# Turned maxima share a ring buffer with the row sums, the FFN runs as one burst, the absolute maximum is taken by halves

## What is computed

```
def proj(W):
    y = jnp.einsum('oc,bct->bto', W, x)
    return y.reshape(B, T, H, Dh).transpose(0, 2, 1, 3)
Q, K, V = (proj(Wq), proj(Wk), proj(Wv))
att = jnp.einsum('bhqd,bhkd->bhqk', Q, K) * (1.0 / math.sqrt(Dh))
att = att + b[0]
m = mask[:, None, None, :]
att = att * m + (1.0 - m) * NEG_INF
att = jax.nn.softmax(att, axis=-1)
y = jnp.einsum('bhqk,bhkd->bhqd', att, V)
...
absmax = jnp.max(jnp.abs(x), axis=-1, keepdims=True)
scale = jnp.maximum(absmax, eps) / 127.0
q = jnp.clip(jnp.round(x / scale), -128, 127).astype(jnp.int8)
...
acc = jnp.einsum('bsk,nk->bsn', q, weight, preferred_element_type=jnp.int32)
out = acc.astype(jnp.float32) * in_scale * w_scale[:, 0] + bias
return out.astype(jnp.float16)
```

## Time and profile before

| | |
|---|---|
| median of 3 runs | 2563.82 us |
| profiled execution, its own time | 2565.66 us |
| its span | 2563.9 us |
| mean granted TensorE clock | 0.991 |
| TensorE, VectorE, ScalarE, GpSimd busy | 96%, 56%, 56%, 72% |
| L131, row maximum 128x1024, x1024 | 1220 ns |
| L911, absolute maximum 128x1024, x32 | 1212 ns |
| L914, L916 (128x1), x32 each | 154, 164 ns |
| L921, product 128x512, x64 | 751 ns |
| L807, exp 128x512, x2048 | 603 ns |
| L974, y 128x512, x64 | 1281 ns |
| L967, addition 128x2048, x254 | 4582 ns |

### The profile page before, as it was taken

The page is one execution under the profiler, slowest core; times in us unless marked ns, Lnnn a source line. Parts: engine busy times, 40 slices in busy tenths (PEclk is TensorE's granted clock), DMA queues, the critical chain, the costliest instruction groups (busy, mean ns, idle before and its releaser), DMA issues.

```text
span 2563.9 us, 40963 instructions
## 1 busy us (share of the span) xinstructions
PE 2455.4 (96%) x12880; PEld 1354.0 (53%) x12880; DVE 1448.3 (56%) x1459; ACT 1435.3 (56%) x2664; POOL 1853.0 (72%) x614
## 2 busy tenths in 40 slices
PE   8999999979999999999999999999999999999996
PEld 7888888864444444444444444444444444444442
DVE  3211111156666666667666666666666666666660
ACT  3222222216656666666666666666666666666664
POOL 3332222227878888888888888888888888888885
PEclk9999999989999999999999999999999999999998
DMA  6655545633333333433333333333333343433311
GB/s 246 255 194 196 196 188 188 207 133 84 89 81 92 89 85 88 95 84 84 84 95 85 84 84 84 84 84 84 84 84 93 92 95 92 90 93 85 86 41 34
DMA packets 151511, 282.62 MB, mean 110 GB/s; under 512 B 30489, under 2 KB 66329, under 8 KB 151393
## 3 DMA queue, kind: packets, MB, share of 16 engines
q10 hardware_dynamic: 49312, 130.80, 22.8%
q1 hardware_dynamic: 102080, 150.57, 16.8%
HBM read 178.29 MB, written 101.45 MB: 109 GB/s over the span
## 4 chain that ended last, share of the span: by engine, by line
PE 58%; DVE 8%; issue 7%; POOL 2%; ACT 2%; DMA 1%; DVEq 0%; ACTq 0%; POOLq 0%; SPq 0%
PE score L703 17%; PE ring L122 16%; PE pv L730 15%; DVE neg_max L131 7%; PE ring L762 4%; PE ring L740 4%; PE ring L743 2%; DVE absmax L911 1%; POOL acc L967 1%; ACT probs L807 1%; POOL y L974 0%; DMA sums<-recips_by_head 0%; DMA recips<-sums 0%; DVE scale L914 0%; POOL k_stack L116 0%
## 5 line engine op out<-in xcount | busy, mean ns | idle before, releaser
L131 DVE TENSOR_REDUCE neg_max<-ring 128x1 f32<-128x1024 f32 x1024 | 1219.0, 1220 | 572.6 <-PE ring L122 570.0
L807 ACT ACTIVATE probs<-score 128x512 f32<-128x512 f32 x2048 | 1104.0, 603 | 378.3 <-PE score L703 357.9
L967 POOL TENSOR_TENSOR acc<-acc,probs 128x2048 f32<-128x2048 f32 x254 | 1163.7, 4582 | 17.4 <-ACT probs L807 0.2
L703 PE MATMUL score<-q_stack,k_stack 100*128 100x512 f32 x2048 | 882.5, 433 | 27.9 <-ACT probs L807 15.2
L122 PE MATMUL ring<-k_stack,q_stack 98*128 98x512 f32 x2048 | 825.1, 403 | 46.3 <-DVE neg_max L131 41.9
L703 PEld LDWEIGHTS score<-q_stack,k_stack 100*128 100x128 f32 x2048 | 387.7, 190 | 489.8 <-ACT probs L807 349.1
L730 PE MATMUL pv<-probs,v_in 128*32 128x512 f32 x4096 | 546.3, 605 | 0.0
L122 PEld LDWEIGHTS ring<-k_stack,q_stack 98*128 98x128 f32 x2048 | 390.6, 191 | 150.3 <-DVE neg_max L131 90.7
L967 POOL TENSOR_TENSOR acc<-probs 128x2048 f32<-128x2048 f32 x64 | 292.6, 4572 | 150.1 <-ACT probs L807 150.1
L474 POOL TENSOR_TENSOR q_stack<-x_raw,k_stack 128x1024 fp32r<-128x1024 f32 x28 | 67.7, 2450 | 293.5 <-ACT k_stack L359 293.5
L730 PEld LDWEIGHTS pv<-probs,v_in 128*32 128x32 f32 x4096 | 80.6, 108 | 185.9 <-issue 106.3
(11 more groups left out here) (90 smaller groups left out, 1888.7 us busy)
## 6 DMA issues: line engine op xcount, KB each, us to landing
k_stack<-qk_part ACTq DMA_DIRECT2D x93, 512.0 KB
q_stack<-qk_part ACTq DMA_DIRECT2D x183, 256.0 KB, 3.9
qk_part<-part_hi SPq DMA_DIRECT2D x64, 512.0 KB, 2.6
qk_part<-part_lo SPq DMA_DIRECT2D x64, 512.0 KB, 3.5
v_steps<-v_out SPq DMA_DIRECT2D x64, 256.0 KB, 2.2
sums<-recips_by_head SPq DMA_DIRECT2D x64, 256.0 KB
res<-x ACTq DMA_DIRECT2D x32, 512.0 KB, 4.5
out<-res SPq DMA_DIRECT2D x64, 256.0 KB, 4.7
```

Source lines behind the costliest of these rows:

```text
L131: nc.vector.tensor_reduce(neg_max[:, pair // CHUNK, pair % CHUNK:pair % CHUNK + 1], ring[:, :], AX_X, ALU.max, negate=True).then_inc(neg_m ...
L703: pe.matmul(score[score_bank(t)][:, :], k_stack[par][0:ROWS, h, kt * P:(kt + 1) * P], q_stack[par][0:ROWS, half, h, :], start=True, stop=T ...
L807: nc.scalar.activation(probs[:, kt, h, :], score[score_bank(t)][:, :], ACT.Exp).then_inc(exp_done, 1)
L967: nc.gpsimd.tensor_tensor(acc[:, half, :, :], first, probs[:, k, :, :], ALU.add).then_inc(acc_done, 1)
```

## The change

- Turned maxima are written to columns 512 to 639 of the ring buffer that takes the sums; sums and turn are one extra: chunk 1 with the sums of (s-1, half 1) at unit 23, chunk 0 of s+1 with the sums of (s, half 0) at unit 55. The turn comes first.
- The turning of q goes from unit 41 to 51. The FFN's 16 matmuls are one extra at unit 59 on both banks of one buffer, with the two products behind them. Extras per step are 4 instead of 7.
- The absolute maximum is taken by halves, at units 27 (with a maximum against EPS, `take_floor`) and 39, and the scale follows there; recip of (s-1, half 1) goes from 17 to 31. round_rows goes from 31, 32 to 41, 42; make_ints from 36, 37 to 43, 44; take_qT from 42, 43 to 52, 53; load_res from 14 to 30.
- SP stores chunk 1 of the maxima ahead of the sums' gather, and gathers (s, half 0) after the store of chunk 0.
- GpSimd: normalise half 0 after the first addition, half 1 after the fourth, finish after the eighth, then two more. The last step adds in half 1 as before.

```diff
-SUMS_1, TURN_1, TURN_Q, FFN_0, FFN_1, SUMS_0, TURN_0 = 11, 23, 41, 45, 49, 51, 55
-EXTRAS = (SUMS_1, TURN_1, TURN_Q, FFN_0, FFN_1, SUMS_0, TURN_0)
+SUMS_1, TURN_Q, SUMS_0, FFN = 23, 51, 55, 59
+EXTRAS = (SUMS_1, TURN_Q, SUMS_0, FFN)
...
             def step(s, par, prev=True, main=True, ahead=True):
-                if prev:
-                    gather_sums(s - 1, 1)
-                    spread_recips(s - 1, 1)
                 if main:
                     sp.wait_ge(max_hi_done, 2 * s + 2)
                     sp.wait_ge(max_lo_done, 2 * s + 2)
                     store_max(par, 1)
-                if main:
-                    gather_sums(s, 0)
+                if prev:
+                    gather_sums(s - 1, 1)
+                    spread_recips(s - 1, 1)
...
-                pe.transpose(buf[0:CHUNK, 0:P], neg_max[:, chunk, :], ident[:, :]).then_inc(maxT_done, 1)
+                pe.transpose(buf[0:CHUNK, N:N + P], neg_max[:, chunk, :], ident[:, :]).then_inc(maxT_done, 1)
...
+            def ffn(s, buf):
+
+                pe.wait_ge(qT_out, 2 * s + 2)
+                for half in range(2):
+                    cols = slice(half * N, (half + 1) * N)
+                    for tt in range(TT):
+                        mm = pe.matmul(buf[:, cols], qT[:, tt, :], fw[:, tt, cols], start=(tt == 0), stop=(tt == TT - 1))
+                    mm.then_inc(ffn_done, 1)
...
+                    if t == SUMS_1 and (prev or main):
+                        buf = take_ring(s, par, use)
+                        if main:
+                            turn_max(s, 1, buf)
+                        if prev:
+                            sum_rows(s - 1, 1, buf)
+                    if t == SUMS_0 and (main or ahead):
+                        buf = take_ring(s, par, use)
+                        if ahead:
+                            turn_max(s + 1, 0, buf)
+                        if main:
+                            sum_rows(s, 0, buf)
...
-                    if t in (31, 32) and prev:
-                        round_rows(s - 1, t - 31)
                     if t == 35 and main:
                         take_y(s, 0)
-                    if t in (36, 37) and prev:
-                        make_ints(s - 1, t - 36)
-                    if t in (42, 43) and prev:
-                        take_qT(s - 1, t - 42, ring_of(par, ("extra", TURN_Q)))
+                    if t in (41, 42) and prev:
+                        round_rows(s - 1, t - 41)
+                    if t in (43, 44) and prev:
+                        make_ints(s - 1, t - 43)
+                    if t in (52, 53) and prev:
+                        take_qT(s - 1, t - 52, ring_of(par, ("extra", TURN_Q)))
...
+            def take_absmax(s, half):
+                dve.wait_ge(y_done, 2 * s + half + 1)
+                nc.vector.tensor_reduce(absmax[:, half:half + 1], y[:, half * N:(half + 1) * N], AX_X, ALU.max,
+                                        apply_absolute_value=True).then_inc(absmax_done, 1)
+
+            def take_floor(s):
+                dve.wait_ge(absmax_done, 2 * s + 1)
+                nc.vector.tensor_scalar(floor[:, :], absmax[:, 0:1], EPS, None, ALU.max).then_inc(floor_done, 1)
+
...
-                    if t == 17 and prev:
+                    if t == SUMS_1 and main:
+                        low_max(s, 1, ring_of(par, ("extra", SUMS_1)))
+                    if t == 27 and prev:
+                        take_absmax(s - 1, 0)
+                        take_floor(s - 1)
+                    if t == 31 and prev:
                         recip(s - 1, 1)
-                    if t == TURN_1 and main:
-                        low_max(s, 1, ring_of(par, ("extra", TURN_1)))
-                    if t == 29 and prev:
+                    if t == 39 and prev:
+                        take_absmax(s - 1, 1)
                         scales(s - 1)
...
                 if main:
-                    for k in range(1, 4):
+                    add(s, 0, 1)
+                if prev:
+                    normalise(s - 1, 0)
+                if main:
+                    for k in range(2, 5):
                         add(s, 0, k)
                 if prev:
-                    for half in range(2):
-                        normalise(s - 1, half)
+                    normalise(s - 1, 1)
                 if main:
-                    for k in range(4, POOLED[0]):
-                        add(s, 0, k)
-                    for k in (1, 2):
+                    add(s, 0, 5)
+                    for k in range(1, 4):
                         add(s, 1, k)
                 if prev:
                     for half in range(2):
                         finish(s - 1, half)
-                if main:
-                    for k in range(3, POOLED[1] if ahead else LAST_POOLED):
+                if main and ahead:
+                    for k in range(4, POOLED):
                         add(s, 1, k)
```

## The result

| | before | after |
|---|---|---|
| median | 2563.16 us (4 runs, 2559.26 to 2564.39) | 2727.15 us (4 runs, 2725.38 to 2739.01) |
| ratio to before | | 1.065 (1.062 to 1.0685) |
| span of the profiled execution | 2563.9 us | 2723.6 us |
| mean granted TensorE clock | 0.991 | 0.953 |
| mean step, steps 3 to 29 | 61.35 us | 66.91 us |

The change makes the kernel 164 us slower, 5.6 us in each step. The sign was forecast, the size was not: 2607 us, with a range that ended at 2647.

The account below looks back on a forecast made before the run. TensorE, 96% busy, was taken as the bound, with its waits to win. Terms -0.6 - 1.0 + 2.6 + 0.5 = +1.5 us a step over 30 steps, +45, ends -2, on 2563.82: 2607 us; range 2556 to 2647.

Parts of the forecast that it names:

- late chain: Reciprocal at unit 31 to absolute maximum at 39: 8.0 us needed against 6.11, TensorE loses 2.6 us a step.
- turned maxima under the sums: At both sum bursts: the reduction ends under the sum matmuls, so the turns' waits go; -0.6 us a step.
- absolute maximum, first half: Moved to unit 27, where it uses VectorE's 0.7 us idle per group with nobody waiting in time; -1.0 us a step.
- turned q: Turn at unit 51: old cost 1.25 us goes, unit 54's row maximum waits 1.37, with transposes 1.8; +0.5 a step.
- FFN as one burst: At unit 59: matmuls take 2 x 1.74 us either way and the products end before unit 62; 0.
- I take 5.08 and keep 6.41 as the upper end: Length in us of the reciprocals' spread, issue to multiplication: kernel-end value taken, in-step value kept as upper end.
- The fit that the prediction took from the Trainium skill: About 2.0 us + bytes / 436e3 per transfer: 2.6 us for the 256 KB spread, in time, which would turn the sign.
- The transpose stays, 0.05 by its place in the step: In the merged sum bursts: each turn's transpose still costs TensorE 0.05 us, giving 2 x (0.05 - 0.34) = -0.6.
- the load of k: Load for the next step: unit 20 comes 2.6 us earlier in the step while DMA engines are full; counted toward slower.
- Rival A: Spread lands in under 3.2 us, VectorE never stands at unit 39: -0.35 us a step, 2551 us; chance 0.15.
- Rival B: Only VectorE's wait is paid, 1.3 instead of 2.6: +0.2 us a step, 2569 us, about no change; chance 0.12.
- Rival C: More contention: the spread meets res and q loads, 6.41 us, +1.33 us a step, 2647 us; chance 0.15.

Follow-up runs that it names:

- e1: The changed kernel with the score matmul of unit 44 issued nine times instead of once: 2663.1 us, ratio 1.0395 to the kernel before.
- e3: The changed kernel with the spread of the reciprocals as four transfers of 64 KB, one per head: 2581.7 us, ratio 1.0088 to the kernel before.
- f1: The changed kernel with the spread per head, second-half absolute maximum at unit 41, rounding at 43 and 45, integers at 47 and 49: 2551.14 us, ratio 0.9965.

## Why the prediction was wrong

The prediction named the late chain, its place and the sign. It went wrong in the size of two terms, and left out a third, the clock. By terms, us per step, the measured ones from the mean unit lengths of steps 3 to 29:

| term | predicted | measured |
|---|---|---|
| turned maxima under the sums | -0.6 | 0.0 (waits of 0.31 gone twice, bursts 2.92 for 2.58 twice) |
| absolute maximum, first half | -1.0 | -0.95 |
| turned q | +0.5 | +0.5 (1.41 before; 0.43 and the wait of 1.49 after) |
| FFN as one burst | 0 | -0.1 |
| late chain, units 43 to 48 at full clock | +2.6 | +3.8 (from e1) |
| TensorE's clock | no term | +2.0 (after less e1) |
| remainder | | +0.3 |
| sum | +1.5 | +5.6 |

*The chain.* The step that failed is "I take 5.08 and keep 6.41 as the upper end". The spread took 5.87 on average, and the steps' own mean before was 5.52. The value from the silent tail was the floor, not the middle. Nor was it quiet around the spread, as the earlier trace rows made it seem: there the share of the DMA engines was 0.20, but during the spread of the kernel after it is 0.48 (second to last number), where the spread alone makes 0.15 from its issue to the multiplication in the silent tail:

```profile
1662.25:1667.80 5.55, 5.55 (x32) 3.03 (x24) 3.46 (x3) 3.77 (x8) 0.43 (x2) 1.00 0.48 123
```

The change itself had moved the load of res, 512 KB, to unit 30. It is issued 3.6 us ahead of the spread (1658.64 in the rows above), where it was 5.7 before, and three loads of q are issued while the spread runs. The prediction gave this move 0. No run put the load back, so its share in the spread's length stays open. From the store's issue to the spread's issue it took 1.69 us in the mean, instead of 1.43. Together this makes VectorE's wait 3.0 us instead of 1.9.

The fit that the prediction took from the Trainium skill (DMA: Bandwidth & Descriptors, "Anatomy of one DMA") stands there for transfers issued from GpSimd, and this one is issued from SP; the 2.6 us that it gave are half of what the spread took in silence.

The rest of the working held: from inv_scale to the score of unit 47 I had 3.7 us, and the trace has 3.7 (1670.2 to 1673.9). The score of unit 47 waited for ScalarE's exp, as argued.

*The clock.* The second step that failed is that the sum has no term for TensorE's clock, and no rival has it. The kernel before keeps full clock with an idle stretch of about 0.7 us in each step, the one inside; the forecast itself put 2.6 us of lost time ahead of the score of unit 47, and I didn't ask what TensorE's clock does behind it. The Trainium skill (TensorE: Matmul & The Clock Gate, "HAM oscillation") warns that idle gaps repeated in a loop bring the half clock back each time; its example has longer waits, for DMA. The trace agrees in the effect, and shows it at a shorter gap: clock 0.51 over the 6.9 us behind a gap of 1.99. That made the loss one and a half times as large, and it makes the cost of a wait uneven: e3 took 2.3 us from the chain and gave 4.7 back.

*The turned maxima.* "The transpose stays, 0.05 by its place in the step" failed. The 0.05 holds where a score follows; between pv and sums the transpose costs 0.34, as much as the waits that it saved. So the part that the change is named after is worth nothing on TensorE, and it is also what binds the sums to unit 23 and leaves the chain so little time.

*What held.* The wait for the turned q (1.37 forecast, 1.49 measured), the FFN, GpSimd (never the bound), SP's order, the load of k (no wait at unit 20). Rival A needed a spread under 3.2 us: 5.87 rules it out. Rival B, that only VectorE's wait is paid (its terms add up to 2568, not 2569), is wrong: the chain cost 3.8 and not 1.3. Rival C, with 6.41 us and 2647, had the chain nearly right, 3.9 for 3.8. It is 80 us short, and the clock is some 60 of them.

## What to carry to other kernels

When work is moved along a fixed order, count the distance between producer and consumer in the slots of the slowest engine and lay the whole round trip beside it, with DMA times from the loaded part of the trace; here 6.1 us were given to 8.8 (from 1660.24 to 1669.07 in the rows above). A wait of 2 us or more that TensorE meets in every step must be priced a second time, by what the clock does behind it; at another place, 1.2 us in every step cost no clock. Before giving up such a change, move the consumer: four units were worth 160 us.

## What the runs showed of the hardware

- The granted clock of TensorE fell to half at or behind an idle stretch of 2.4 us in the mean, once in nearly every step, and stayed there 6.6 us in the mean. Eight redundant matmuls in the stretch made the kernel 64 us faster; four left 22 of 29 low stretches; eight elsewhere left 23 and made it slower. In f1 an idle stretch of 1.2 us in every step, at another place, went with one low stretch in all.
- A spread of 256 KB onto 128 partitions took, from its issue to the use of what it brings, 5.9 us in the loaded step and 5.1 in silence as one transfer with 4 in its outermost dimension, and 3.5 as four transfers with 32, in spite of three more issues on SP.
- A 128x128 transpose between two groups of 32-column matmuls cost 0.34 us on TensorE, and 0.03 behind them.
